# A Perceiver block on one core: order of the work at the first loads, around the router rows, and at the last additions

## The reference, cut to what matters

```python
x = x + xattn(layernorm(x), mask, ctx, ctx)     # softmax(q k^T / 32 + mask) v
x = x + attn(layernorm(x))                      # 16 heads, 4 kv heads, rope, causal
x = x + ffn(layernorm(x))
# xattn: the last 512 rows of keys and values are x Wk + bk, x Wv + bv
# attn:  out = y_out @ Wproj + y_out @ p_A @ p_B,  y_out = y less its part along v
# ffn:
logits  = einsum('th,eh->te', x, router_weight)          # 16 experts
combine = two best experts of the two best groups, weights normed to sum 1
a       = relu2(einsum('th,ehi->tei', x, w_up)) * combine
routed  = einsum('tei,eih->th', a, w_down)
shared  = relu2(x @ shared_up) @ shared_down             # 1024 -> 2048 -> 1024
return routed + shared
```

## Time and profile before

| | |
|---|---|
| median of 3 runs | 1433.86 us (1431.6 to 1434.49) |
| profiled execution, its own time | 1433.06 us |
| its span, first to last instruction | 1431.2 us |
| PE busy | 1402.1 us, 98% |
| DVE busy | 851.7 us, 60% |
| ACT busy | 530.0 us, 37% |
| POOL busy | 192.6 us, 13% |
| mean granted clock of PE | 0.997 |

### The profile page before, as it was taken

One profiled execution on the slowest core, in us unless ns is written; L12 is line 12 of the kernel. 1 busy time (PEld: TensorE's weight loads), 2 busy tenths in 40 slices (PEclk: granted clock), 3 DMA queues, 4 the chain that ended last, 5 costly groups with the idle time before them and its releaser, 6 DMA issues. The chain is left out here.

```text
span 1431.2 us, 18183 instructions
## 1 busy us (share of the span) xinstructions
PE 1402.1 (98%) x6676; PEld 1148.8 (80%) x6676; DVE 851.7 (60%) x1236; ACT 530.0 (37%) x951; POOL 192.6 (13%) x264
## 2 busy tenths in 40 slices
PE   6999999999999999999999999999999999999998
PEld 5878888888888888888888888867777788888886
DVE  5655455455555455555545557576877576777665
ACT  3222232223322222332222322555643335666561
POOL 3000100000000000000000000253432013112022
PEclk9999999999999999999999999999999999999999
DMA  6444543333333333333333231400110456988765
GB/s 232 150 188 169 217 186 118 131 112 115 112 110 112 123 125 110 117 110 110 114 125 121 82 132 66 148 1 1 60 34 1 147 176 210 333 297 293 263 237 206
DMA packets 43630, 203.63 MB, mean 142 GB/s; under 512 B 5249, under 2 KB 5313, under 8 KB 32129
## 3 DMA queue, kind: packets, MB, share of 16 engines
q1 hardware_dynamic: 29296, 149.17, 29.7%
q0 software_dynamic: 9568, 36.35, 8.0%
q10 hardware_dynamic: 4704, 17.30, 3.1%
HBM read 182.36 MB, written 20.45 MB: 142 GB/s over the span
## 5 line engine op out<-in xcount | busy, mean ns | idle before, releaser
L32 PE MATMUL banks<-V_hi,b_PT_hi 128*128 128x512 f32 x512 | 205.6, 401 | 0.0
L1041 ACT ACTIVATE b_PT_hi<-banks 128x512 fp32r<-128x512 f32 x64 | 38.3, 598 | 446.7 <-PE banks L773 446.7
L34 PE MATMUL banks<-V_hi,b_PT_lo 128*128 128x512 f32 x512 | 200.2, 391 | 0.0
L33 PE MATMUL banks<-V_lo,b_PT_hi 128*128 128x512 f32 x512 | 199.6, 390 | 0.0
L34 PE MATMUL banks<-K_hi,QT_lo 128*128 128x512 f32 x512 | 199.4, 389 | 0.0
L32 PE MATMUL banks<-K_hi,QT_hi 128*128 128x512 f32 x512 | 199.3, 389 | 0.0
L33 PE MATMUL banks<-K_lo,QT_hi 128*128 128x512 f32 x512 | 199.2, 389 | 0.0
L1281 DVE TENSOR_TENSOR b_scores<-banks,b_scores 128x512 f32<-128x512 f32 x64 | 44.2, 691 | 199.1 <-PE banks L34 199.1
L656 POOL DMA_DIRECT2D b_scores<-mask x60 | 32.2, 537 | 638.5 <-PE banks L773 626.4
L2225 DVE TENSOR_TENSOR e_lo<-e_raw,e_hi 128x1024 fp32r<-128x1024 f32 x80 | 97.2, 1254 | 31.1 <-ACT e_hi L2049 30.3
L34 PEld LDWEIGHTS banks<-V_hi,b_PT_lo 128*128 128x128 f32 x512 | 96.1, 188 | 21.0
(11 more groups left out here) (329 smaller groups left out, 2742.8 us busy)
## 6 DMA issues: line engine op xcount, KB each, us to landing
raw<-kv SPq DMA_DIRECT2D x60, 1024.0 KB, 4.7
e_raw<-w_up SPq DMA_DIRECT2D x40, 512.0 KB, 5.5
e_raw<-w_down SPq DMA_DIRECT2D x40, 512.0 KB, 6.2
b_scores<-mask POOLq DMA_DIRECT2D x64, 256.0 KB, 2.9
d_s_raw<-shared_w SPq DMA_DIRECT2D x26, 512.0 KB, 4.3
raw<-xattn_w SPq DMA_DIRECT2D x11, 1024.0 KB, 4.9
y_dram<-c_zeros ACTq DMA_DIRECT2D x1, 6656.0 KB, 27.0
raw<-attn_w SPq DMA_DIRECT2D x6, 1024.0 KB, 4.7
```

The lines of the kernel that those rows point to most:

```text
L32: pe.matmul(out, lhs_hi, rhs_hi, start=first, stop=False)
L33: pe.matmul(out, lhs_hi, rhs_lo, start=False, stop=False)
L34: return pe.matmul(out, lhs_lo, rhs_hi, start=False, stop=last)
L1041: act.activation(PT_hi[:, u % 2, :], T_ps[:, u % 2, :], ACT.Copy).then_inc(b["pt_hi"], 1)
```

## The change: what it does

Three places are edited.

1. The first tile of x is loaded in one transfer of 128 x 1024 instead of two of 128 x 512. Its statistics wait for the whole tile. The semaphore `x_first` goes.
2. `output(7)` follows `output(6)` at once, and `turn_xn(2)` comes behind both. `route_rows` before `turn_xn(3)` covered tokens 128 to 511 and all eight blocks; now tokens 256 to 511 and blocks 0 to 3 come before `turn_xn(3)` and blocks 4 to 7 behind it. The rest, behind the last low parts, was tokens 0 to 127 and is now 0 to 255. On ACT the first two `shared_hi` come ahead of `xn_hi(4)`, on DVE the two `shared_lo` ahead of `xn_lo(4)`; `xn_lo(4)` and `xn_lo(5)` now lie behind `add_out(7)` and its statistics, one on each side of `third_norm(3)`.
3. At the end DVE takes the tiles in turn: the two expert rows of a tile, then its two units. The stores of tiles 0 to 2 wait for the tile's units, no longer for its expert rows alone.

```diff
-            for h in range(2):
-                sp.dma_start(resid[:, 0, h * W:(h + 1) * W],
-                             ins["x"][0][:, h * W:(h + 1) * W]).then_inc(x_loaded[0] if h else x_first, 16)
+            load_x(0)
...
-            dve.wait_ge(x_first, 16)
-            ln.half_stats(dve, resid, stats, 0, 0)
-            dve.wait_ge(x_loaded[0], 16)
-            ln.half_stats(dve, resid, stats, 0, 1)
-            ln.aggregate(dve, 0, stats, mean_var, 0)
+            x_stats(0)
...
-def route_rows(pe, out, F, first, last):
+def route_rows(pe, out, F, first, last, blocks=range(DB)):
-    for e in range(DB):
+    for e in blocks:
...
             output(6, 0, DB)
+            output(7, 0, DB)
             turn_xn(2)
-            output(7, 0, DB)
-            pe.wait_ge(d["xt_lo_done"], 6)
+            pe.wait_ge(d["xt_lo_done"], 4)
             pe.wait_ge(d["rw_split"], 1)
-            route_rows(pe, bank[:, Y_BANK, :], F, P, T)
+            route_rows(pe, bank[:, Y_BANK, :], F, 2 * P, T, range(4))
             turn_xn(3)
+            route_rows(pe, bank[:, Y_BANK, :], F, 2 * P, T, range(4, DB))
...
             pe.wait_ge(s["xt_lo_done"], 2 * TB)
-            route_rows(pe, bank[:, LOGIT_BANK, :], F, 0, P).then_inc(s["logits_ready"], 1)
+            route_rows(pe, bank[:, LOGIT_BANK, :], F, 0, 2 * P).then_inc(s["logits_ready"], 1)
...
             for t in range(TB - 1):
-                act.wait_ge(s["add_done"], t + 1)
+                act.wait_ge(s["unit_added"], 24 + 2 * t + 2)
                 act.dma_start(out[t], resid[:, t, :]).then_inc(s["out_stored"], 16)
...
-                        dve.wait_ge(s["unit_added"], 24 + 2 * min(t + 1, TB - 1))
+                        dve.wait_ge(s["unit_added"], 24)
...
-            for n in range(40, 43):
-                add_unit(n)
-            add_rows(0)
-            add_unit(43)
-            add_rows(1)
-            add_unit(44)
-            add_unit(45)
-            add_rows(2)
-            add_rows(3)
-            dve.wait_ge(s["add_done"], TB)
-            for n in range(46, 48):
-                add_unit(n)
+            for t in range(TB):
+                add_rows(t)
+                dve.wait_ge(s["add_done"], t + 1)
+                add_unit(40 + 2 * t)
+                add_unit(41 + 2 * t)
```

More of the change, by code:

```diff
@@ L113, in cross_projections @@
     x_loaded = [m.sem(f"a_x_loaded{t}") for t in range(TB)]
-    x_first = m.sem("a_x_first")
     bias_loaded = m.sem("a_bias_loaded")
@@ L1208, in _ @@
             act.activation(F["rw_pair"][:, :, 0:E], F["rw"], ACT.Copy).then_inc(d["rw_hi_done"], 1)
+            shared_hi(0)
+            shared_hi(1)
             xn_hi(4)
             xn_hi(5)
-            shared_hi(0)
-            shared_hi(1)
             xn_hi(6)
@@ L1542, in _ @@
             half_stats(3, 0)
-            xn_lo(4)
-            xn_lo(5)
             shared_lo(0)
@@ L1548, in _ @@
             half_stats(3, 1)
+            xn_lo(4)
             third_norm(3)
+            xn_lo(5)
             xn_lo(6)
@@ L2185, in _ @@
                 act.wait_ge(s["unit_added"], 31 + c)
-                act.wait_ge(s["add_done"], TB)
                 act.dma_start(out[TB - 1][:, c * W:(c + 1) * W],
```

## The result

The changed kernel takes 1428.46 us (median of 18 runs, 1426.27 to 1430.77), the kernel before 1433.84 in as many runs beside it (1431.33 to 1435.38). The ratio is 0.9963, 95% interval [0.9956, 0.9970]: 5.4 us or 0.37% faster. The profiled execution of the changed kernel took 1429.72 us, its span is 1427.8. It is thus only 3.3 us shorter than the one of before (1433.06), though the medians are 5.4 apart: this execution had falls of PE's clock that some others of the same kernel did not have.

The account below looks back on a forecast made before the run. PE, busy 98% of the span, was taken as the bound. Gains of 0.2 (start), 3.8 (router rows) and 1.2 (end) sum to 5.2 us: 1427.9 from the profiled 1433.06, 1428.7 from the median; stated 1428.1, range 1426.2 to 1431.2.

Parts of the forecast that it names:

- What bounds the kernel: Whole kernel: PE busy 98% of the span; gains only in its 29 us idle, half-pace stretches, or after its last matmul.
- the forecast's own list of signs: What the profile should show, including DVE's end 1.3 us behind PE's last matmul instead of 2.7.
- The middle: Around the router rows: 3.8 us gained, 3.1 from the clock and 0.7 from the order; bounds 3.2 to 4.0.
- The reason given for the clock: Router rows: clock stays up because matmuls are wider, 256 columns, and stand on both sides of the transposes; real doubt admitted.
- the clock's gain would carry into the time: After the router rows: nothing later eats the 3.8 us, since routing, splits and gathers follow PE's progress.
- The start: First rows, tile 0 in one load: 0.2 us gained, between -0.5 and +0.4.
- the transfers and not the issue set it: Start: tile 1's arrival is set by the same bytes in front, so the saved 0.43 us issue may gain nothing.
- The rival of the late start: Start: whole tile 0 moves as slowly as tile 1, everything 2 us later, 1430.1 us; chance 0.05.
- The last additions: Kernel's end, DVE taking expert rows first: 1.2 us gained, between 0 and 1.5.
- run in the midst of the gathers: End: stores of tiles 0 and 1 are issued 2.2 and 1.5 us earlier, among the gathers; 1.2 us gain taken.
- The rival by which the gathers give the end back: End: interleaved stores make e_y land 1.4 us later, DVE waits; 1429.1 us with the clock held; chance 0.11.
- no row here shows two queues sharing: End: no profile row showed queues sharing DMA engines, so stores slowing gathers at once stayed only a rival.

Follow-up runs that it names:

- e3: Only the tail edit (expert rows taken tile by tile ahead of the last units) on the kernel before; 1432.95 us, ratio 1.0005.
- e12: Changed kernel with unit 44's add moved, tile 0's store held back, position counts split, and sixteen router matmuls joined ahead of the last transposes; 1427.63 us, 0.9951.
- e4: Only the middle edit on the kernel before, with the sixteen router matmuls of tokens 256 to 511 joined ahead of the last transposes; 1430.37 us, 0.9983.
- e2: Only the middle edit (projections in a row, router rows in two halves about the last transposes) on the kernel before; 1430.53 us, 0.9979.
- e1: Only the start edit (tile 0 of x in one load) on the kernel before; 1433.03 us, 0.9999.
- e5: Kernel before, with tile 0 of x in two loads of 64 whole rows instead of two of half rows; 1434.27 us, 1.0004.
- e8: Changed kernel with the position counts' narrow matmuls split, six ahead of unit 3 and eight behind it; 1427.54 us, 0.9960.
- e10: Changed kernel with the first ten of the position counts' narrow matmuls done twice; 1433.96 us, 1.0000.
- e9: Changed kernel with only tile 0's store held back to tile 1's last add; 1427.58 us, 0.9957.
- e11: Changed kernel with unit 44's add ahead of tile 2's rows, tile 0's store held back to tile 1's, and position counts split around unit 3; 1425.95 us, 0.9945.
- e7: Changed kernel with the stores of tiles 0 to 2 held back to tile 2's last add; 1427.18 us, 0.9966.

## Why the prediction was right, and where it was not

The forecast of 1428.1 is 0.4 us from the median. It was itself a choice: the sum of 5.2 us gives 1427.9 from the profiled execution and 1428.7 from the median, and the measured 1428.46 lies between. Its terms are not equally good.

- **What bounds the kernel** was read rightly: PE's busy time did not move (1402.1 us both, with equally long falls), and what was won lies in PE's idle time, in its clock and behind its last matmul. One reading was off: DVE's end was put at "some 2.3 us behind PE", and by the rows it is 2.7, as the forecast's own list of signs has it.
- **The middle: right in path and sizes.** It forecast 3.8 us, of it 0.7 from the order and 3.1 from the clock. The table has 27.25 before, 24.00 for the old order at full clock (e3) and 23.26 after: 0.74 and 3.25. The details held too: 256 columns took 0.12 us (0.13 forecast), the idle pieces were 1.67 and 0.63 us (1.8 and 0.8), and with the 1.23 added by which tile 1's transposes came earlier the logits' transposes stand at 1122.32, 0.2 from the 1122.55 forecast. The reason given for the clock is neither shown nor refuted. The forecast trusted to the wider matmuls. They aren't enough to keep the clock in every run, since e12 has them and falls; but e4, with them and without the halves, is as fast as e2 (1430.37 and 1430.53). Which part of the new order keeps the clock up, the width, the halves or the projection moved forward, no run here separates.
- **That the clock's gain would carry into the time** was taken as sure, and is only mostly so. The fall at the router rows is gone from nine profiles of the ten with part 2 (e12 is the exception), but two other places have one in some executions, behind the position counts and at 936. Both are old: e1 and e5, with the old order, have them too. In the medians 5.4 less the 2.8 without the clock leave 2.6 for it, against 3.1 forecast. At full clock, nine runs of before took 1428.36 to 1430.58 (median 1429.53) and four of after 1426.27 to 1426.98 (1426.74), 2.8 apart.
- **The start: the term was mis-sized, 0.2 for 1.5.** PE starts at 9.31 to 10.04 in five profiles with two loads (mean 9.64) and at 7.75 to 8.46 in nine with one (mean 8.12). This lies outside the forecast's own bounds of -0.5 to 0.4. The step that failed is "the transfers and not the issue set it": the bytes in front are the same, but with two loads of half a tile DVE waits for tile 1 until 8.49 (before) or 8.09 (e5), and with one it is there by 5.68. The rival of the late start had the sign wrong.
- **The last additions: 1.2 forecast, 0.55 won** (0.2 to 0.55 by the four profiles after, e3, e8 and e10). The step that failed is the store's place in the sum. That the stores "run in the midst of the gathers" was seen, and priced at 0.2; it costs DVE 1.24 us (after against e9). The rival by which the gathers give the end back was true in its mechanism, but named the wrong pair: `e_y` came in time and tile 2's `d_s_raw` did not, since in the new order DVE asks for them at 1416.25, 1.2 us ahead of their landing. POOL's longer first gather instruction (1.78 us against 0.98) had taken the 0.8 us of slack that the rows of before would have left. It stood in no term. Without the store the term would have been 3.12 - 1.33 = 1.8. The rule that each DMA engine alternates between its queues (the Trainium skill, "DMA: Bandwidth & Descriptors", section "Queues, rings and completion order") now has its rows: landings of 5.8, 6.9 and 7.7 us beside the store, 5.2, 5.5 and 5.6 without it. The trace of before had such a row already, against the forecast's "no row here shows two queues sharing": ACT issued a store of 0.5 MB at 1417.61 while `e_y`'s gather was under way, and that is the gather with 7.9 us.
- **The sum** came out by two errors that cancel: the start 1.3 us too small, the tail 0.65 and the clock 0.5 too large. That the median came so near is luck in that measure. The terms that the runs show, 1.5 + 0.74 + 0.55, make 2.8, as the runs at full clock do.

What stays open: what keeps the clock up at the router rows; what brings the fall at 936, in four profiles of fourteen, where no edit was aimed; why a tile in two loads is slower than in one; and how e11's 2.5 us over the changed kernel divide, since each of e7, e8 and e9 alone is within the scatter of five runs from after. As an estimate, its median lies 0.8 under the full-clock runs of after (1426.74), which is what the three edits win without the clock, and 1.7 is then the clock.

## What to carry to other kernels

Where the engine that bounds a kernel is 98% busy, look for stretches in which it is busy at half pace, and for what it did just before: an edit there can be worth far more than the idle time it takes away (here 0.74 us of order came with 3.25 of clock). A row of very narrow matmuls is such a place; with wide ones put into it, no fall followed in three profiles, and no cost showed. A transfer that is issued earlier is not free: ask which transfers it now runs beside, and who waits for these. An issue that takes longer beside another engine's work can use up the slack of all behind it. And compare distances within the profiles part by part before the times, since two single executions can differ by a fall of the clock that has nothing to do with the edit.

## What the runs showed of the hardware that was not expected

- PE's clock fell with PE busy without a gap, inside a row of matmuls of 16 columns (e10: from 1.00 to 0.50 at 1143.3, behind some 3.3 us of them). There, busy time in the profile doesn't tell such a stretch from dense work.
- The falls seen between the first and last matmul lasted 3.41 or 6.83 us, in all nine profiles that have any.
- A tile of 512 KB was there for use at 4.23 us in one load; in two loads of 64 rows it was there at 5.73. PE started at 9.64 us on average in the five profiles with two loads of either kind, and at 8.12 in the nine with one.
- POOL's gather instruction took 1.78 us where it began 0.36 us into DVE's row additions (two operands in SBUF), and 0.93 to 0.98 in the gathers behind it; in the kernel before it is `e_y`'s that took 1.62, begun 0.46 us into such additions. The Trainium skill ("SBUF — State Buffer", section "SBUF: two separate sides") has GpSimd and DVE share a port pair, which one holds for a whole instruction; one such wait fits the 0.8 us, but the later gathers ran beside DVE's additions too and did not show it, so no run here settles it.
